# The opening of an attention and feed-forward kernel: first q/k tiles in the scores' banks, roots of two tiles at once, first head's scores without copies; even pairs' normals one place later

## The reference, cut to what matters

```python
B, S, D, H, DH = 8, 512, 256, 16, 64          # x is (8, 512, 256), f32
x = x + layernorm(attn(layernorm(x)))
x = x + layernorm(ffn(layernorm(x)))
# attn: q, k, v = x @ w_q, x @ w_kv, per head of 64 columns
#   q = q / |q| * exp(scale[h]);  k = k / |k|
#   out = softmax(q k^T) v;  out @ w_out + b_out
# ffn: h = silu(x w1^T s1) * (x w2^T s2); two gelu layers 1024 -> 1024 (h1, h2); h w3^T s3
```

## Time and profile before

| | |
|---|---|
| median of 3 timed runs | 1758.13 us (1755.85 to 1760.71) |
| profiled execution, its own time | 1754.84 us |
| its span, first to last instruction | 1753.0 us |
| PE busy | 1701.9 us, 97% |
| DVE, ACT, POOL busy | 1179.5 us, 1009.9 us, 497.6 us |
| chain that ended last | 76% PE, 10% DVE, 6% DMA |

### The profile page before, as it was taken

One profiled execution on the slowest core, in us unless ns is written; L12 is line 12 of the kernel. 1 busy time (PEld: TensorE's weight loads), 2 busy tenths in 40 slices (PEclk: granted clock), 3 DMA queues, 4 the chain that ended last, 5 costly groups with the idle time before them and its releaser, 6 DMA issues.

```text
span 1753.0 us, 24640 instructions
## 1 busy us (share of the span) xinstructions
PE 1701.9 (97%) x8578; PEld 1414.8 (81%) x8578; DVE 1179.5 (67%) x2022; ACT 1009.9 (58%) x1350; POOL 497.6 (28%) x561
## 2 busy tenths in 40 slices
PE   5999999999999999999999998999999999999998
PEld 4778888888878888888888886888888888888877
DVE  5777887887877887887887885545454545544454
ACT  4777777777777777777777775322323141323231
POOL 3533543543543543543543540000000000000000
PEclk9999999999999999999999999999999999999999
DMA  4546546546546546546546654400000000000000
GB/s 129 121 113 163 135 115 164 133 117 164 131 115 163 133 118 163 131 115 157 116 108 152 175 138 105 166 13 24 1 25 1 25 1 24 1 25 1 25 1 24
DMA packets 76780, 163.41 MB, mean 93 GB/s; under 512 B 28272, under 2 KB 28656, under 8 KB 76656
## 3 DMA queue, kind: packets, MB, share of 16 engines
q1 hardware_dynamic: 67296, 128.64, 30.9%
q10 hardware_dynamic: 8352, 29.50, 5.7%
q0 software_dynamic: 1008, 3.67, 0.5%
HBM read 68.97 MB, written 20.19 MB: 51 GB/s over the span
## 4 chain that ended last, share of the span: by engine, by line
PE 76%; DVE 10%; DMA 6%; issue 4%; ACT 2%; POOL 2%; SPq 1%; DVEq 0%; ACTq 0%; POOLq 0%
PE bank L1044 15%; PE pair L1121 13%; PE pair L1122 13%; PE bank L986 11%; PE pair L1027 5%; PE pair L1028 4%; PE bank L1058 4%; PE pair L1111 3%; PE pair L1112 3%; DVE Pl L705 3%; DMA rows<-Rp 3%; PE bank L1013 2%; PE bank L1138 2%; PE bank L1139 2%; DMA work<-rows 1%
## 5 line engine op out<-in xcount | busy, mean ns | idle before, releaser
L1121 PE MATMUL pair<-hh,f 128*128 128x512 f32 x1024 | 399.4, 390 | 0.7 <-DVE hl L819 0.2
L1122 PE MATMUL pair<-hl,f 128*128 128x512 f32 x1024 | 398.6, 389 | 0.0
L1044 PE MATMUL bank<-Ph,V 128*128 128x512 f32 x1024 | 366.5, 399 | 17.4 <-DVE Pl L705 12.4
L493 ACT ACTIVATE P<-pair,sh 128x1024 f32<-128x1024 f32 x256 | 286.6, 1119 | 152.3 <-PE pair L1028 136.9
L705 DVE TENSOR_TENSOR Pl<-P,Ph 128x1024 fp32r<-128x1024 f32 x256 | 313.9, 1226 | 3.1 <-ACT Ph L498 3.0
L986 PE MATMUL bank<-w,xh 128*128 128x256 f32 (+1 forms) x1024 | 289.2, 345 | 6.8 <-DVE turned L699 2.8
L543 ACT ACTIVATE hr<-pair,ct 128x512 f32<-128x512 f32 x128 | 88.3, 690 | 357.7 <-PE pair L1122 357.7
L498 ACT ACTIVATE Ph<-P 128x1024 fp32r<-128x1024 f32 x256 | 271.7, 1062 | 8.1
L1044 PEld LDWEIGHTS bank<-Ph,V 128*128 128x128 f32 x1024 | 193.4, 189 | 75.1 <-issue 23.3
L1121 PEld LDWEIGHTS pair<-hh,f 128*128 128x128 f32 x1024 | 192.2, 188 | 43.8 <-DVE hl L819 3.5
L1122 PEld LDWEIGHTS pair<-hl,f 128*128 128x128 f32 x1024 | 192.2, 188 | 39.8
(11 more groups left out here) (104 smaller groups left out, 2608.7 us busy)
## 6 DMA issues: line engine op xcount, KB each, us to landing
stack<-turned SPq DMA_DIRECT2D x128, 384.0 KB, 4.3
stack<-turned SPq DMA_DIRECT2D x128, 256.0 KB, 4.8
work<-rows SPq DMA_DIRECT2D x128, 128.0 KB, 2.9
raw<-in_h ACTq DMA_DIRECT2D x16, 512.0 KB, 5.0
xr<-in_h ACTq DMA_DIRECT2D x16, 512.0 KB, 3.6
f<-raw ACTq DMA_DIRECT2D x12, 512.0 KB, 5.6
f<-raw SPq DMA_DIRECT2D x10, 512.0 KB, 10.5
xt<-in_x SPq DMA_DIRECT2D x8, 512.0 KB, 4.4
```

Source lines behind the costliest of these rows:

```text
L493: e.activation(M.P[:, i % 2, :], M.SB[i % 2][:, :], ACT.Exp, bias=M.sh[:, h:h + 1]).then_inc(S["exp"])
L1044: d = e.matmul(M.OB[:, :], v, p[:, u % 3, j * 512:(j + 1) * 512], start=jt == 0 and m == 0, stop=jt == 3 and m == 2)
L1121: e.matmul(ps, w, M.hh[src][:, k, :].bitcast(to), start=k == 0, stop=False)
L1122: d = e.matmul(ps, w, M.hl[src][:, k, :].bitcast(to), start=False, stop=k == KH - 1)
```

## The change

- **Opening.** x of batch 0 comes in two halves with a semaphore each, and the statistics of the first half start with it. PE issues 20 transposes of the identity into the output bank before the first real ones and 6 after them. The first four q/k tiles go to the four halves of `SB` (`FB`), without a wait for a bank. `ss` and `rs` hold four tiles; POOL takes the roots of tiles 0 and 1 at once, then of 2 and 3 (`first_roots`, 16 columns). PE does both first pieces of v and tile 4 before the first `turn`, which waits tile by tile. Two of the four splits of `w_out` move from places 12 and 13 into the opening, ahead of the first `square` on ACT and the first `head_sums` on DVE; the other two stay at places 5 and 6.
- **First head.** `scores(0)` and `scores(1)` read the turned halves directly with 6 matmuls of 64 rows each; only the odd head of pair 0 is copied. `turn_high(1)` waits for `scores(1)`.
- **Quads.** On DVE the odd pair's `turn_low` moves from place 1 to the end of place 0. The even pairs' `normal` moves from place 1 to the end of place 2, their `o_low` from place 2 to the end of place 3, their `o_high` on POOL to place 3. On SP the stack copies at place 6 go ahead of `take_sums`. On ACT the weight copies move from place 7 to place 0.
- **End.** `normal(60)` goes from place 249 to the end of place 252, `normal(61)` from place 253 to behind the last `p_low`; `outp` of quad 30 moves behind the second group of the feed-forward part.

```diff
-    for t in range(NT):
-        square(t)
-    v_high(0)
+    split_wo(0)
+    split_wo(1)
+    square(0)
+    square(1)
     split_w(2)
+    square(2)
+    square(3)
+    split_w(3)
+    v_high(0)
+    v_high(1)
+    square(NT)
     turn_high(0, 1)
     turn_high(0, 0)
...
+    def first_roots(u):
+        ss, rs = (v[:, u:u + 2, :].rearrange("p a b -> p (a b)") for v in (M.ss, M.rs))
+        q.wait_ge("ssum", u + 2)
+        e.tensor_scalar_max(ss, ss, TINY).then_inc(S["smax"], 2)
+        q.wait_ge("smax", u + 2)
+        e.tensor_tensor(rs, ss, M.half[:, :], ALU.pow).then_inc(S["rs"], 2)
+        q.wait_ge("rs", u + 2)
+        q.wait_ge("eq", 3)
+        for t in (u, u + 1):
+            e.tensor_tensor(M.rs[:, t, :], M.rs[:, t, :], M.eq[:, 0, :, :, :].rearrange("p b c d -> p (b c d)"),
+                            ALU.mult).then_inc(S["rq"])
...
+    def turn_idle(n):
+        q.wait_ge("c1", 1)
+        for _ in range(n):
+            e.transpose(M.OB[:, 0:128], M.ident[:, :], M.ident[:, :])
...
+        if g == 0:
+            for name in ("thk", "thq", "tlk", "tlq"):
+                q.wait_ge(name, 1)
+            for j in range(2):
+                ps, own = M.SB[i][:, j * 512:j * 512 + 512], slice((2 * c + j) * 128, (2 * c + j + 1) * 128)
+                e.matmul(ps, M.turned[0:64, 1, own], M.turned[0:64, 2, :], start=True, stop=False)
+                e.matmul(ps, M.turned[0:64, 0, own], M.turned[0:64, 2, :], start=False, stop=False)
+                d = e.matmul(ps, M.turned[0:64, 1, own], M.turned[0:64, 3, :], start=False, stop=True)
...
+    q.wait_ge("x0", 16)
+    turn_idle(20)
     x_turn(0, 0)
     x_turn(0, 1)
+    turn_idle(6)
     for t in range(NT):
         qk_tile(t)
     v_tiles(0)
+    v_tiles(1)
+    qk_tile(NT)
     turn(0, 1)
     turn(0, 0)
-    v_tiles(1)
-    qk_tile(NT)
...
+def normal_slot(n):
+    return {NP - 4: NU - 4, NP - 3: NU + 1, NP - 2: NU + 1, NP - 1: NU + 5}.get(n, 4 * n + 10 - n % 2)
...
+        if r == 2 and 0 <= n - 3 < NP and normal_slot(n - 3) == i:
+            normal(n - 3)
+        if i == normal_slot(NP - 4):
+            normal(NP - 4)
+        if r == 3 and 0 <= n - 3 < NP and low_slot(n - 3) == i:
+            o_low(n - 3)
...
+    normal(NP - 3)
+    o_low(NP - 3)
     normal(NP - 2)
```

More of the change, by code:

```diff
@@ L86, in bank_plan @@
 def bank_plan():
-    order = [(u, -2) for u in [("x", 0), ("x", 1)] + [("qk", t) for t in range(NT)]]
-    order += [(u, -1) for u in [("v", 0), ("Tk", 0), ("Tq", 0), ("v", 1), ("qk", NT)]]
+    order = [(u, -2) for u in [("x", 0), ("x", 1), ("v", 0), ("v", 1)]]
+    order += [(u, -1) for u in [("qk", NT), ("Tk", 0), ("Tq", 0)]]
     for i in range(SLOTS):
@@ L112, with qk_bank, copies @@
 PLAN = bank_plan()
+def qk_bank(M, u):
+    return M.FB[u] if u < NT else M.G[PLAN["qk", u][0]][:, :]
+def copies(n, odd):
+    return 16 * (n // 2 + (1 if n % 2 or odd else 0))
 def wait_bank(q, user):
@@ L185, with low_slot @@
 COUNTS = (19,) + tuple(32 * b + r for b in range(7) for r in (23, 27, 31))
-def copy_at(i):
-    n, r = divmod(i - 15, 8)
-    return n if r == 0 and 0 <= n < PIECES else None
+RAWS = tuple(8 * q for q in range(1, 28) if q < 8 or q % 4 != 3)
+def normal_slot(n):
+    return {NP - 4: NU - 4, NP - 3: NU + 1, NP - 2: NU + 1, NP - 1: NU + 5}.get(n, 4 * n + 10 - n % 2)
+def low_slot(n):
+    return NU - 2 if n == NP - 4 else normal_slot(n) + 1
 def grp(b, n, m):
@@ L297, in sync_program @@
         e.dma_start(dst, src).then_inc(S["cst"], 16)
-    for odd in (0, 1):
-        stack(0, odd)
+    for k in (2, 3):
+        load_wo(k)
+    stack(0, 1)
     for i in range(SLOTS):
@@ L302, in sync_program @@
         i32_, pb = i % 32, i // 32 - 1
-        if i in (5, 6):
-            load_wo(i - 3)
+        if i % 8 == 6 and pair_of(i - 1) is not None:
+            stack(pair_of(i - 1), 1)
         if i % 2 == 0 and 0 <= i // 2 - 2 < NG:
@@ L312, in sync_program @@
             stack(pair_of(i), 0)
-        late = 2 if i % 8 == 2 else 1
-        if i >= late and i % 8 in (2, 6) and pair_of(i - late) is not None:
-            stack(pair_of(i - late), 1)
+        if i % 8 == 2 and pair_of(i - 2) is not None:
+            stack(pair_of(i - 2), 1)
         if i % 4 == 3 and 0 <= i // 4 - 1 < NP:
@@ L405, in pool_program @@
     norm_root(0)
-    for t in range(NT + 1):
-        head_root(t)
+    first_roots(0)
+    first_roots(2)
+    head_root(NT)
     for i in range(SLOTS):
@@ L468, in square @@
     def square(u):
-        bank = PLAN["qk", u][0]
         q.wait_ge("qk", u + 1)
         q.wait_ge("ssum", u)
-        e.activation(M.sq[:, :], M.G[bank][:, :], ACT.Square).then_inc(S["sq"])
+        e.activation(M.sq[:, :], qk_bank(M, u), ACT.Square).then_inc(S["sq"])
     def v_high(n):
@@ L616, in wait_stacked @@
             for part in range(2):
-                q.wait_ge(f"k{n % 2}{odd}{part}", 16 * (n // 2 + 1))
+                q.wait_ge(f"k{n % 2}{odd}{part}", copies(n, odd))
 def vector_program(q, M):
@@ L852, in vector_program @@
     scales()
+    split_wo(0)
+    split_wo(1)
     head_sums(0)
[L854 to L857, removed]
+    head_sums(1)
+    split_w(2)
+    head_sums(2)
+    head_sums(3)
+    head_scale(0)
+    head_scale(1)
+    split_w(3)
     v_low(0)
-    split_w(2)
+    head_scale(2)
+    head_scale(3)
+    v_low(1)
     turn_low(0, 1)
     turn_low(0, 0)
-    split_w(3)
-    v_low(1)
     head_sums(NT)
@@ L875, in vector_program @@
             p_low(i - 1)
-        if r == 1 and pair_of(i - 1) is not None:
-            turn_low(pair_of(i - 1), 1)
-            turn_low(pair_of(i - 1), 0)
+        if i == NU - 7:
+            turn_low(NP - 1, 1)
+            turn_low(NP - 1, 0)
         if i < 3:
             split_w(4 + i)
-        if i in (5, 6, 12, 13):
-            split_wo(i - 5 if i < 7 else i - 10)
-        if i % 4 == 2 and 0 <= n - 3 < NP:
+        if i in (5, 6):
+            split_wo(i - 3)
+        if r == 6 and 0 <= n - 3 < NP and low_slot(n - 3) == i:
             o_low(n - 3)
-        if i % 4 == 1 and 0 <= n - 3 < NP:
+        if i == low_slot(NP - 4):
+            o_low(NP - 4)
+        if r == 5 and 0 <= n - 3 < NP and normal_slot(n - 3) == i:
             normal(n - 3)
@@ L901, in vector_program @@
             v_low(values_of(i))
-        if r == 5 and pair_of(i) is not None:
+        if pair_of(i) is not None and i != NU - 8:
             turn_low(pair_of(i), 1)
@@ L1146, in layers @@
                 group(b, n, m, rounded)
-                if b == 0 and n == 1 and m == 1:
-                    outp(NQ - 1, 0)
-                    outp(NQ - 1, 1)
+                if b == 0 and n < 2 and m == 1:
+                    outp(NQ - 2 + n, 0)
+                    outp(NQ - 2 + n, 1)
         if b + 1 < B:
```

73 lines of the change are left out of this document (37 added, 36 removed).

## The result

The changed kernel takes 1788.8 us (1784.7 to 1789.5) against 1758.3 (1755.9 to 1760.7): ratio 1.0169, interval 1.0148 to 1.019. It is about 30 us slower; forecast was 1753.0, range 1742 to 1763. Its profiled execution took 1784.67, span 1782.9.

The account below looks back on a forecast made before the run. PE was taken as the bound, busy 97% of the span. Opening 10.2 won, quads 4 and end 3 lost make 3 faster: 1751.8 from the profiled execution or 1755.1 as median, put at 1753.0 us, range 1742 to 1763.

Parts of the forecast that it names:

- normals and low halves, quads and end: Moved DVE work in the quads and last places: net 4 us lost in the quads, 3 lost at the end.
- `turn_low` at place 0: DVE, place 0 in place of 1: stands ahead of a p_low with over 1 us of slack, so costs nothing.
- opening: Start of the kernel, place 8 and places 12 to 15: first score at 29.2, 6.3 earlier; 10.2 us won in all.
- later `take_sums` (two issues) ahead of a `normal` that now comes 4 us later: nothing: SP at place 6 of a quad: issuing the sums' transfer behind the stack copies costs nothing.
- The quads' loss: Moved normal and o_low delay p_low: 1.8 + 0.4 + 0.5 = 2.7 us a batch, 19 for seven batches.
- The 1.8: Second quads: PE waits 1.8 us for p_low in place of 0.37.
- The wait named for place 47: Second quad of a batch: PE already waits 0.37 us there, forecast to become 1.8.
- the 15 us of old waits: Quads: late normals and copies that place 0 waits for go away, with the half clock behind them: 15 us won.
- a wait of over 2 us costs again that much behind it: PE's clock: after such a wait it runs at half clock, losing as much again.
- The end: Last places: 2 us won on the stack copy, waits of 2.7 for evacuate(124), about 4 for evacuate(126); 3 lost.
- that rival: DVE becomes the bound in every quad, each of 30 paying one o_low of 0.7 us: 18 slower, 1771; chance 0.12.
- The clock rival: Opening: the 26 idle transposes bring no full clock, costing 0.6 to 1 us, 1754; chance counted within the forecast's 0.50.

Follow-up runs that it names:

- e1: The changed kernel with SP issuing take_sums ahead of the odd head's stack copies again, as before the change; 1756.5 us, ratio 0.9984.
- e8: e3 plus the low halves of turned at place 0, the weight copies at place 0 and the moved outp; 1737.1 us, ratio 0.989.
- e12: The kernel before with 16 columns allotted for the exponent in place of 8, only 8 used; 1750.1 us, ratio 0.9951.
- e14: The kernel before with 16 columns allotted for the exponent and the low halves of turned at place 0, without the new opening; 1744.3 us, ratio 0.9918.
- e10: e3 plus only the low halves of turned at place 0, ahead of p_low; 1738.7 us, ratio 0.9891.
- e7: e3 plus the moved normals and the low and high halves of O, those of the last pairs too; 1767.3 us, ratio 1.0058.
- e3: The kernel before with only the opening and first head of the change; 1743.2 us, ratio 0.9906.
- e4: e3 plus the changed order on SP, the odd head's stack copies ahead of take_sums at place 6; 1816.5 us, ratio 1.0314.
- e9: The changed kernel with invert moved from the end of place 7 to place 0 behind p_low; 1770.8 us, ratio 1.0076.
- e6: e3 with the sums and roots in rings of two again from the fifth tile on; 1744.9 us, ratio 0.9926.
- e11: The kernel before with 16 exponent columns and rings of four for sums and roots allotted, none of the new columns used; 1750.3 us, ratio 0.9943.
- e5: e3 without the 26 idle transposes; 1745.2 us, ratio 0.9907.
- e17: The kernel before with 80 columns allotted for the exponent, 288 bytes more, and nothing else; 1750.7 us, ratio 0.9954.
- e13: The kernel before with 24 columns allotted for the exponent, 64 bytes more, and nothing else; 1756.2 us, ratio 0.9995.
- e16: The kernel before with 32 columns allotted for the exponent, 96 bytes more, and nothing else; 1756.5 us, ratio 0.9990.

## Why the prediction was wrong

By differences of ratios (times 1758 us; each has 3 to 5 us of uncertainty, so the terms of 4.7 and 5.8 are hardly clear of nothing):

| term | forecast | measured | from |
|---|---|---|---|
| SP: stack ahead of `take_sums` | 0 | +32.5 | after against e1 |
| normals and low halves, quads and end | +7 | +16.5 | e1 against e8 |
| start of the tiles in SBUF | not in the sum | -8.6 | e12 |
| `turn_low` at place 0 | 0 | -5.8 | e14 against e12 |
| opening | -10.2 | -4.7 | e10 against e14 |
| weight copies, `outp` | 0 | 0 | e8 against e10 |

They add up to the measured 29.7, but for 0.2 of rounding, because they are differences along one row of kernels from after to before; that is no test of them. Each price holds beside the others as they then stood: the normals alone cost 27 (e7 against e3), and SP's order 73 (e4 against e3).

**The step that failed** is the half sentence on the "later `take_sums` (two issues) ahead of a `normal` that now comes 4 us later: nothing". It asked the last reader of the sums and not the first. That is `invert`, at the end of DVE's place 7, and what is queued behind it is `add_part`, whose bank PE's `turn` takes at place 0, and the `p_low` of `values`. In the kernel before `invert` already waited 3.4 us in 8 places, so there at least it had no slack; that row was there to read. e1 shows the cause, e9 the way: with the transfer as late but `add_part` and `p_low` no longer behind the wait, 23 of the 26.9 us of the quads are back. Dp is issued 2.65 us later against its place, and at place 232 it is not there 7.4 us after its issue; with the sums first it was in time 5.1 after. So at this place the transfer itself is slower too; its median over the quads is 4.7 us from issue to landing, 4.1 with the sums first.

**The quads' loss was right, the gain beside it was not.** By place, e1 against e8, the normals cost 0.7 us in a first quad, 1.5 in a second, 0.0 in a third and 0.7 in a fourth (means of batches 1 to 6): 2.9 a batch, forecast 2.7, in the forecast's order (0.4, 1.8, 0, 0.5). The 1.8 was a wait in place of one of 0.37, so 1.4 more; with that the forecast's own sum is 2.3 a batch. The wait named for place 47 stands in the changed kernel. The first two rows are the moved `normal` and the moved `o_low`; the `normal` at 221.45 is the odd pair's, which stands there before the change too:

```profile
211.02 1.39 DVE L759 TENSOR_TENSOR work<-work 64x512 f32<-64x512 f32 x2
...
215.67 0.71 DVE L765 TENSOR_TENSOR nl<-work,nh 128x512 fp32r<-128x512 f32 x1
...
221.45 2.36 DVE L759 TENSOR_TENSOR work<-work 64x512 f32<-64x512 f32 x2
223.84 1.29 DVE L737 TENSOR_TENSOR turned<-bank,turned 128x512 fp32r<-128x512 f32 x2
225.05 1.21 DVE L743 TENSOR_TENSOR Pl<-P,Ph 128x1024 fp32r<-128x1024 f32 x1
...
226.41 0.47 PE L1114 MATMUL bank<-Ph,V 128*128 128x512 f32 x1 [0.88 <-DVE Pl L743]
```

From 211.02 to this p_low DVE has no pause in which to catch up. The wait is 0.88, not 1.8; in second quads the loss is 0.3 us each at places 4 and 5 and 0.6 and 0.5 at places 6 and 7. The term that failed is the 15 us of old waits credited to the moves: with the normals moved (e7 against e3) no place of a quad gains as much as 0.1 us in the mean of batches 1 to 6. Some of those waits come and go from kernel to kernel with the normals as before: PE's wait for p_low is 12.4 us in 17 in the kernel before, 4.9 in 8 in e3 and 11.8 in 15 in e10.

**`turn_low` at place 0** was judged by what it delays, a p_low with slack, and not by what it hastens: the bank for PE's projection at place 1. By the ratios it gives 5.8 (e14 against e12) or 2.6 (e10 against e3).

**The opening**: the power took 2.94 (3.0 forecast), the first score came at 30.4 (29.2), 5.2 earlier instead of 6.3. Of the 1.2 us missing, 0.7 are POOL's first maximum, which took 0.94 (0.2 put). Place 8 waits 1.74, not 1.4. A single pair of executions doesn't price the whole: e10 is 6.6 us ahead of e14 at place 24, 1.3 at place 248 and 4.9 at place 255. The means at place 24 are 131.1 (e3, e6, e8, e10) and 136.1 (e11, e12, e14, e17), so 5.0, near the 4.7 of the ratios. 10.2 was too much. Its price for a pause, "a wait of over 2 us costs again that much behind it", fails in its own rows: behind the wait of 2.43 a matmul takes 0.76 us at a granted clock of 0.50, but behind that of 2.67 the one at 44.05 takes 0.47, and the clock from 44 to 47 us is 1.00.

**The end**: PE waits 3.60 for `evacuate(124)` (2.7 forecast) and 1.92 for `evacuate(126)` (4):

```profile
1096.97 0.77 PE L1114 MATMUL bank<-Ph,V 128*128 128x512 f32 x1 [3.60 <-ACT work L537]
...
1108.48 0.47 PE L1114 MATMUL bank<-Ph,V 128*128 128x512 f32 x1 [2.09 <-issue]
...
1112.04 0.47 PE L1114 MATMUL bank<-Ph,V 128*128 128x512 f32 x1 [1.92 <-ACT work L537]
```

What ended the 2.09 between them the profile doesn't name. Places 248 to 255 take 27.4 in e1 and 23.0 in e8: 4.4 lost, forecast 3; e7 against e3 gives 4.1.

**The rivals.** DVE did become the bound, and by more than that rival's 18 us, but through a transfer for which its queue stands, more than through the moved operations. The clock rival: the idle transposes do bring the full pitch, so its mechanism is wrong here; its price (0.6 to 1 us) doesn't show, since the first square waits for the load of w_out and not for the tiles (e5). The Trainium skill, "TensorE: Matmul & The Clock Gate", Part 4 (PE-mode transpose), has it that transposes do not count as activity as matmuls do; e3 against e5 shows 0.23 against 0.43 us, so here the measurement says otherwise.

## What to carry to other kernels

For a transfer that is issued later, look for the first instruction that waits for it and list everything behind that in its engine's queue, not only the last reader. A move is to be priced for what it hastens too: freeing a bank 0.2 us sooner was worth 3 to 6 us over 31 quads. And a change of a small tile's size moves all tiles behind it; compare with the kernel before at the same places before crediting a gain to the edit. e8 (1737.1, e10 as fast) keeps what paid: the opening, the halves at place 0 and the wider exponent, with the sums first and the normals where they were.

## What was not expected of the hardware

**The start of the tiles.** With the same instructions, 0.5% (8 to 10 us) hang on where the large tiles from `turned` on begin: at a multiple of 256 bytes they gain it (e11, e12, e17), at 32 or 64 past it nothing that shows (e13, e16). In e11 the instructions of PE, DVE and ACT take as long as before, within 2%. By place, 3.4 of the 4.3 us that e12 gains in batches 1 to 6 lie at place 3 of the fourth quads, where PE in the kernel before waits for a `p_low` behind a late `normal`, as the one of the earlier trace rows. The Trainium skill, "DMA: Bandwidth & Descriptors", How a descriptor splits into AXI transactions, says that a transaction must begin at a multiple of 256 bytes and that the bytes from there to the descriptor's start are fetched for nothing. A boundary of 256 agrees with the runs, which don't tell it from one of 128. If the cost went by the bytes fetched for nothing, 32 past would be far better than 224, and e13 is as slow as the kernel before. Which transfers are slower, and by how much, the traces don't settle: the medians from issue to landing of the stack copies lie between 4.2 and 4.8 us in all of them.

**The clock.** The stretch of the first tiles in e3 and in e5: us, busy time of PE, PEld, DVE, ACT and POOL, granted clock, DMA share, GB/s.

```profile
11.70:17.20 5.50, 5.49 (x24) 4.60 (x25) 2.40 (x7) 2.07 (x4) 0.00 (x0) 1.00 0.54 189
```

```profile
11.90:16.40 4.50, 4.43 (x11) 3.50 (x12) 1.60 (x7) 1.71 (x3) 0.00 (x0) 1.00 0.62 221
```

The granted clock reads 1.00 in both, though one has 24 matmuls in 5.5 us and the other 11 in 4.5. The second reading is empty: e5's trace has no clock record before 16.43 us (e3's begin at 9.43), and the column counts a stretch without one as 1.00. There the level, 1.2 or 2.4 GHz, shows in the distance between matmuls, which changes from 0.43 to 0.23 at 16.4. Ahead of the first stretch PE ran the 26 idle transposes and the 8 real ones, ahead of the second only the 8.
